# A gated delta rule with an FP4 feed-forward on one core: beta put into the decays, the last output norm on VectorE and ScalarE, and four weight strips decoded before the constants

## The reference

```python
beta = sigmoid(xn @ b_w.T + b_bias + beta_bias) * 2.0            # per row and head
g = -exp(A_log) * softplus(xn @ a_w.T + dt_bias)                 # log of the decay
def step(S, inp):                                                # one row, 16 heads
    q_t, k_t, v_t, g_t, b_t = inp
    S = S * exp(g_t)
    mem = einsum('bhk,bhkv->bhv', k_t, S)
    delta = (v_t - mem) * b_t
    S = S + einsum('bhk,bhv->bhkv', k_t, delta)
    return S, einsum('bhk,bhkv->bhv', q_t, S)
o = o * rsqrt(mean(o * o, axis=-1) + eps)                        # the output norm
o = (o * silu(g_out)) @ o_w.T
# ffn: h = silu(x @ gate) * (x @ up), weights FP4 with scales; y = h @ down; y / rms(y)
```

## Time and profile before

| what | value |
|---|---|
| median of 3 runs | 3336.32 us (3335.82 to 3341.81) |
| profiled execution, its own time | 3332.51 us |
| its span, first to last instruction | 3330.7 us |
| mean granted clock of PE | 0.988 |
| busy: PE, DVE, POOL, ACT | 3142.1, 2390.6, 1918.8, 1667.4 us |
| matmul records | 45632 |
| one step of the loop, from tile to tile | about 101 us |

### The profile page before, as it was taken

How to read it: one execution, slowest core, us unless ns; L and a number is a source line. 1 busy time by engine, 2 the same in 40 slices (tenths; PEclk the granted TensorE clock), 3 DMA queues, 4 the chain that set the end, 5 groups by cost and what they waited for, 6 DMA issues and landing times.

```text
span 3330.7 us, 118645 instructions
## 1 busy us (share of the span) xinstructions
PE 3142.1 (94%) x45632; PEld 2252.9 (68%) x45632; DVE 2390.6 (72%) x5408; ACT 1667.4 (50%) x3306; POOL 1918.8 (58%) x2865
## 2 busy tenths in 40 slices
PE   5999999999999999999999999999999999999995
PEld 4666766766666766666767767667667666767663
DVE  7677776777776777777777767777767777767772
ACT  3544554544554545554445545445545455544452
POOL 4566555666555665556665556665556655556652
PEclk8999999999999999999999999999999999999996
DMA  3111111111111111111111111111111111111111
GB/s 112 39 46 27 37 43 33 46 45 28 34 43 36 46 37 27 43 37 42 46 27 37 43 33 46 46 27 37 43 33 46 40 28 39 42 37 46 34 25 30
DMA packets 318318, 132.08 MB, mean 40 GB/s; under 512 B 277089, under 2 KB 278881, under 8 KB 317793
## 3 DMA queue, kind: packets, MB, share of 16 engines
q1 hardware_dynamic: 313824, 119.26, 14.3%
q10 hardware_dynamic: 4096, 6.42, 0.5%
HBM read 75.30 MB, written 50.33 MB: 38 GB/s over the span
## 4 chain that ended last, share of the span: by engine, by line
PE 77%; DVE 12%; issue 6%; POOL 2%; ACT 1%; ACTq 1%; DMA 1%; DVEq 0%; SPq 0%; POOLq 0%
PE PS L1166 17%; PE PS L1122 13%; PE PS L1153 8%; PE PS L1235 7%; PE PS L1154 7%; PE PS L1376 6%; DVE arena L893 4%; PE PS L1221 3%; PE PS L1300 2%; PE PS L1253 2%; DVE arena L378 2%; PE PS L1271 2%; PE PS L1391 2%; DVE arena L988 1%; PE PS L1178 1%
## 5 line engine op out<-in xcount | busy, mean ns | idle before, releaser
L893 DVE SCALAR_TENSOR_TENSOR arena<-PS,sc,arena 128x256 f32<-128x256 f32 x2112 | 1001.0, 482 | 253.0 <-ACT arena L613 152.2
L1153 PE MATMUL PS<-xh,wgu 128*128 128x256 f32 x2816 | 871.6, 341 | 35.9 <-DVE arena L893 35.4
L613 ACT ACTIVATE arena<-PS,sc 128x256 f32<-128x256 f32 x704 | 330.0, 474 | 759.0 <-PE PS L1154 700.3
L1154 PE MATMUL PS<-xl,wgu 128*128 128x256 f32 x2816 | 698.8, 282 | 0.0
L1166 PE MATMUL PS<-wdn,inner 128*128 128x512 f32 x1408 | 650.7, 592 | 0.0
L1153 PEld LDWEIGHTS PS<-xh,wgu 128*128 128x128 f32 x2816 | 531.2, 189 | 155.8 <-issue 84.2
L511 POOL TENSOR_TENSOR work<-arena 128x31 f32<-128x31 f32 (+15 forms) x992 | 511.9, 516 | 137.5 <-DMA arena<-scr_a 62.3
L515 POOL TENSOR_TENSOR arena<-arena,work 128x31 f32<-128x31 f32 (+15 forms) x992 | 542.1, 546 | 77.7
L1154 PEld LDWEIGHTS PS<-xl,wgu 128*128 128x128 f32 x2816 | 530.4, 188 | 83.2 <-issue 83.2
L1122 PE MATMUL PS<-xnT,wqkv 128*128 128x256 f32 x2048 | 485.6, 388 | 25.2 <-ACT inner L593 15.4
L1122 PEld LDWEIGHTS PS<-xnT,wqkv 128*128 128x128 f32 x2048 | 383.6, 192 | 93.1 <-ACT inner L593 16.4
(11 more groups left out here) (147 smaller groups left out, 4619.2 us busy)
## 6 DMA issues: line engine op xcount, KB each, us to landing
xt<-in_x SPq DMA_DIRECT2D x64, 256.0 KB, 2.8
scr_a<-arena SPq DMA_DIRECT2D x64, 256.0 KB, 2.4
arena<-scr_a SPq DMA_DIRECT2D x256, 64.0 KB, 3.2
obuf<-in_x SPq DMA_DIRECT2D x64, 256.0 KB, 2.8
scr_t<-arena SPq DMA_DIRECT2D x32, 512.0 KB, 2.7
arena<-scr_t SPq DMA_DIRECT2D x256, 64.0 KB, 2.3
out<-obuf SPq DMA_DIRECT2D x64, 256.0 KB, 2.0
wqkv<-in_wqkv ACTq DMA_DIRECT2D x1, 2048.0 KB, 14.3
```

The lines of the kernel that those rows point to most:

```text
L613: eng.activation(fa[:, u % 4, :], PS[:, bank(u, 0), 0:NB * P], ACT.Copy, scale=sc[:, u % 2, KB * m:KB * m + 1]).then_inc(fa_scaled.sem, 1)
L893: eng.scalar_tensor_tensor(out=fa[:, u % 4, :], in0=PS[:, bank(u, k // 2), k % 2 * NB * P:][:, 0:NB * P], scalar=sc[:, u % 2, KB * m + k:K ...
L1153: eng.matmul(o, w, xh[:, k, :], start=True, stop=False)
L1154: ins = eng.matmul(o, w, xl[:, k, :], start=False, stop=True)
```

## The change

Three edits at once.

1. Beta leaves the keys and becomes a factor of E. POOL multiplies E by beta, two instructions of 128x512, in a new `decays_with_beta` between `rest_of_x` and `next_tile`; `gram_products` waits for them. DVE loses the ckb multiply of each batch. PE loses `turn_kb`, and `turn_kqn(1)` takes its place in the order. ACT copies the plain keys of batch b in `masked_keys(b)` in place of `other_keys`.
2. In the last step alone the output norm moves from POOL to DVE (gate and scale) and ACT (logarithm and exponential in place of the power).
3. DVE decodes strips 0 to 3 in a row and makes the constants' products behind them.

```diff
+        def decays_with_beta(eng, n):
+
+            hold(eng, *beta_part.at(n, 3))
+            hold(eng, *decay_done.at(n, NB))
+            for b in range(NB):
+                eng.tensor_tensor(E[:, b, :, :], E[:, b, :, :], bc(bet[:, b, :], CH), ALU.mult).then_inc(e_scaled.sem, 1)
...
                 rest_of_x(eng, n)
+                decays_with_beta(eng, n)
                 next_tile(eng, t, n)
                 keys_for_state(eng, t, n)
-            if t:
+            if t and n:
                 gated_and_scaled(eng, t)
...
                 eng.wait_ge(*kqn_turned.at(n, b + 1))
+                eng.activation(kbT[:, b, :, :].rearrange("p f t -> p (f t)"), PS[:, 6, 2 * P:4 * P],
+                               ACT.Copy).then_inc(kb_copied.sem, 1)
...
-            def other_keys():
...
+            def last_roots():
+
+                eng.wait_ge(*so_done.at(t, NB))
+                eng.activation(ro[:, :, :], so[:, :, :], ACT.Ln, scale=1.0 / DV, bias=epso[:, :]).then_inc(ro_done.sem, 1)
+                eng.preload_act_table_set(EXP)
+                eng.wait_ge(*ro_done.at(t, 1))
+                eng.activation(ro[:, :, :], ro[:, :, :], ACT.Exp, scale=-0.5).then_inc(ro_done.sem, 1)
...
             u_rows(3)
-            other_keys()
+            masked_keys(1)
             gate_copy(0)
             gate_copy(1)
-            masked_keys(1)
...
                 put(eng, kqn[:, b, :].rearrange("p (h d) -> p h d", d=DK), rows(b), cn[:, b, :]).then_inc(qk_part.sem, 1)
-                put(eng, kbq[:, b, 0:C // 2].rearrange("p (h d) -> p h d", d=DK), rows(b)[:, H:, :],
-                    ckb[:, b, :]).then_inc(qk_part.sem, 1)
...
-                eng.wait_ge(*decay_done.at(n, b + 1))
+                eng.wait_ge(*e_scaled.at(n, b + 1))
...
             if not n:
+                for b in range(NB):
+                    eng.wait_ge(*gs_done.at(t, 1))
+                    eng.tensor_tensor(sq[:, b, :], sq[:, b, :], gs[:, b, :], ALU.mult).then_inc(o_gated.sem, 1)
+                for b in range(NB):
+                    eng.wait_ge(*ro_done.at(t, 2))
+                    eng.wait_ge(*o_gated.at(t, b + 1))
+                    oh = sq[:, b, :].rearrange("p (h v) -> p h v", v=DV)
+                    eng.tensor_tensor(oh, oh, bc(ro[:, b, :], DV), ALU.mult).then_inc(o_scaled.sem, 1)
...
-            for i in range(2):
+            for i in range(KB):
                 decode(eng, i)
             eng.wait_ge(consts_loaded.sem, 16 * 11)
...
-            for i in range(2, KB):
-                decode(eng, i)
...
-            turn_kb()
+            turn_kqn(1)
...
             p_times_u(0)
-            turn_kqn(1)
             turn_q()
```

More of the change, by code:

```diff
@@ L130, in build @@
         eps = sb("eps", [P, 1])
+        epso = sb("epso", [P, 1])
         mhalf = sb("mhalf", [P, NB, H])
@@ L213, in build @@
         gx_done = signal("gx_done", 2)
+        e_scaled = signal("e_scaled", 2)
         exs_moved = signal("exs_moved", 1)
@@ L243, in build @@
         knq_copied = signal("knq_copied", 4)
-        kb_copied = signal("kb_copied", 1)
+        kb_copied = signal("kb_copied", 2)
         q_copied = signal("q_copied", 1)
@@ L272, in build @@
         coef_done = signal("coef_done", 6)
-        qk_part = signal("qk_part", 4)
+        qk_part = signal("qk_part", 2)
         qk_done = signal("qk_done", 2)
@@ L303, in build @@
         kqn_turned = signal("kqn_turned", 2)
-        kb_turned = signal("kb_turned", 1)
         q_turned = signal("q_turned", 1)
@@ L665, in masked_keys @@
                                    ACT.Copy, scale=par[:, e:e + 1]).then_inc(knq_copied.sem, 1)
-            def other_keys():
-                if not n:
-                    return
-                eng.wait_ge(*kb_turned.at(n, 1))
-                eng.activation(kbT[:, :, :, :].rearrange("p b f t -> p (b f t)"), PS[:, 6, :], ACT.Copy).then_inc(kb_copied.sem, 1)
             def queries():
@@ L755, in act_step @@
             decay(1)
+            if not n:
+                eng.preload_act_table_set(LOG)
             u_rows(2)
@@ L777, in act_step @@
             unit(3)
-            eng.preload_act_table_set(SILU)
             if n:
+                eng.preload_act_table_set(SILU)
                 gate(0)
@@ L791, in act_step @@
             if not n:
+                last_roots()
                 o_columns()
@@ L826, in _ @@
             eng.preload_act_table_set(EXP)
-            eng.wait_ge(zeroed.sem, 4)
+            eng.wait_ge(zeroed.sem, 5)
             first = Tile(0, 0, first=True)
@@ L1078, in _ @@
             eng.memset(halo[:, :, :, :], 0.0).then_inc(zeroed.sem, 1)
+            eng.memset(epso[:, :], float(np.finfo(np.float32).eps)).then_inc(zeroed.sem, 1)
             eng.memset(S[:, :, :, :, :], 0.0).then_inc(zeroed.sem, 1)
@@ L1309, in turn_kqn @@
                 if b:
-                    eng.wait_ge(*kb_copied.at(n, 1))
+                    eng.wait_ge(*knq_copied.at(n, 2))
                 else:
@@ L1315, in turn_kqn @@
                 ins.then_inc(kqn_turned.sem, 1)
-            def turn_kb():
-                if not n:
-                    return
-                eng.wait_ge(*qk_done.at(n, NB))
-                eng.wait_ge(*knq_copied.at(n, 2))
-                for m in range(4):
-                    ins = eng.transpose(PS[:, 6, m * P:(m + 1) * P], kbq[:, m // 2, m % 2 * P:(m % 2 + 1) * P], ident[:, :])
-                ins.then_inc(kb_turned.sem, 1)
             def turn_q():
@@ L1342, in gram @@
                 hold(eng, *knq_copied.at(n, 2 * (b + 1)))
-                hold(eng, *kb_copied.at(n, 1))
+                hold(eng, *kb_copied.at(n, b + 1))
                 if b:
```

## The result

The changed kernel takes 3348.28 us (median of 17 runs, 3343.91 to 3350.50), the one before 3339.85 us on the same chip (17 runs, 3335.50 to 3345.04). The ratio is 1.0023, 95% interval 1.0016 to 1.0031: slower, by 8 us, where the prediction had 28. The profiled execution after took 3344.44 us with a span of 3342.6, against 3332.51 and 3330.7 before: +11.9.

What follows compares the result with a forecast made beforehand. PE bounds 78 us of a step, DVE the other 22. Steps +40 (30 x 1.33 - 0.2 + 0.3), start -6.2 and last step -5.4 gave +28 on the profiled 3332.51; time given as 3363 us, range 3328 to 3388.

Steps and rivals of the forecast that it cites:

- The picture of two stretches: One loop step: PE sets the pace for 78 us, DVE for the 22 us before it.
- a microsecond on either is a microsecond a step: PE's part up to k_times_u(3) and DVE's part from there: time added or saved on either counts fully.
- The toll, "1.55 us later": In state(3), POOL's E multiplies hold DVE's updates of S, so the layer norm's apply starts 1.55 us later.
- E0: POOL's first E multiply (E1 the second), behind rest_of_x: from 1686.26 to about 1687.5, 0.18 lost to the update.
- The ckb multiply leaves DVE: In products(0), PE's 0.23 us wait for DVE goes: a gain of 0.22 us a step, not 0.84.
- turn_kb leaves PE: Four transposes go behind p_times_u(0), where PE waits anyhow: 0; worth 0.6 if that cover were gone.
- A step, +1.33: Each of 30 loop steps gets longer: 1.55 us of toll less 0.22 for the ckb multiply.
- The step with n = 31: No layer norm ahead, so rest_of_x and E are done before state(3): only -0.2 us.
- Rival 4: PE's granted clock drops when its idle time in the 22 us grows to 5; adds to the forecast; chance 0.05.
- Start and end: Ahead of the loop, earlier strips give -6.2 us; in the last step, the norm off POOL gives -5.4.
- Rival 2: Half the toll in state(3), 0.9 us, as DVE's second update slips in before E0: +9, 3345; chance 0.15.
- Rivals 1 and 3: State(3): no toll, 3317, chance 0.2; or POOL does both E multiplies in a row, 2.2 a step, 3384, chance 0.1.

Runs made afterwards that it cites:

- e7: The changed kernel with both E multiplies behind conv(6) and POOL's rest_of_x moved ahead of layer_norm_scale; ratio to before 0.9921, 3305.03 us.
- e3: The changed kernel with POOL's two E multiplies moved behind the last convolution, conv(6); ratio to before 0.9934, 3312.83 us.
- e5: The changed kernel with only batch 1's E multiply moved behind conv(6), batch 0's left in place; ratio to before 0.9999.
- e10: e7 with turn_kqn(1) and ScalarE's copy of it back at their places of before, behind p_times_u(0); ratio to before 0.9921.
- e6: e3 with four small memsets added at the start of VectorE's program, which only shift its later instructions; ratio to before 0.9945.
- e8: e7 with four small memsets added at the start of VectorE's program; ratio to before 0.9931.

## Why the prediction came out as it did

*The picture of two stretches* held: the 78 us did not change, the loop's loss lies in the 22 us, and the small gain at products(0). But "a microsecond on either is a microsecond a step" is only half true. It holds for a microsecond more on VectorE; for 1.6 fewer, e7 shows a gain of 0.11. The prediction read DVE's chain without a hole as DVE alone being late, and didn't ask how close the next engine was. The nine additions give it away: 4.78 before, in the mean as in the earlier trace rows, and 4.59 for the same nine in every step after. The 0.20 were small waits for ScalarE behind PE, and they came back once DVE was later; in e3, where it is not, they are there (4.75).

*The toll, "1.55 us later"*: this is the step that failed, as a size: it measured 1.19. Together with the 0.20 us that came back in the additions it is why a step forecast at +1.33 came out at +0.67. The mechanism is right, in its place, its order (one update let through per multiply) and its condition (two SBUF operands; the masked multiply out of PSUM passes). Two terms of its working were wrong. "0.18 lost to the update": E0 starts 2.31 us behind rest_of_x's start and lasts 1.04, so POOL loses nothing while DVE's held update finishes 0.08 behind it. "The first update of batch 1 then waits for E1 (1687.5 to 1688.7)": E1 starts with E0's end, 1.00 us behind E0's start, while DVE is at its held update and the masked multiply, and nearly half of it is over when that update arrives (0.48 of 1.05 us). Worked out with this, from rest_of_x's start: its end, 2.35, two multiplies at 1.00 start to start, 0.08, and the last update's 0.19 make 4.62, where the last update of S ends in the trace at 4.63 and in before at 3.46: 1.17. e5 splits the same sum into 0.81 and 0.36. The Trainium skill (SBUF — State Buffer, Who interferes with whom) calls the shared port pair an exclusive lock that the first to issue has for the whole instruction; the trace agrees (held updates end 0.08 us behind POOL's instruction), and shows beside it that at an instruction's end the waiting one gets in at no cost to the other engine.

*"The ckb multiply leaves DVE", -0.22*: right. PE's wait for products(0) went from 8.5 us to 0.8, and from the start of y_times_s(0) to the end of k_times_u(3) the mean fell from 17.65 to 17.43.

*"turn_kb leaves PE", 0*: right against before (k_times_u(3) ends 4.98 behind k_times_u(2) before, 4.96 after), and e10 shows beside it that the place of the other set is worth 0.02. What the four transposes are worth with the cover gone, 0.6 by the prediction, was not tried by itself. Of the 0.44 us a step that e3 gains on before, 0.39 lie between the end of the down products and the next k_times_u(3) (mean 37.92 to 37.53), and some 0.2 of these in the part from y_times_s(0) on, where the ckb multiply was waited for; the rest, ahead of it, comes and goes between kernels (e6 doesn't have it) and is open.

*A step, +1.33*: in means over the 29 steps, 1.19 at apply, +1.00 left at the end of the additions, +0.96 at the end of the down products, and -0.29 behind them, in all +0.67. PE's idle time in the 22 us, forecast at about 5, is 3.67. Of the 0.66 that the forecast is above it, 0.36 is the toll's size and 0.20 the small waits that came back; the remaining 0.10 is spread thin.

*The step with n = 31, "only -0.2"*: wrong by the 4.6 us above the usual toll. That rest_of_x and E are done before state(3) there is right. What happened, a stop of 2.23 us in DVE's issue and the clock that followed, no row of before could have told. It goes with the code's position, as e6 and e8 show (103.53 in place of 106.45, 102.88 in place of 106.50). Not all of the 4.6 is this stop: 3.4 lie in chunks 1 and 2, behind it, and 1.4 ahead of y_times_s(0), where PE has a stop on "issue" of 1.09 us of its own (0.2 less elsewhere); the memsets take away 2.9 and 3.6, and what is left in e6 and e8 is open. That the stop is an instruction fetch is argued from the times of the transfers beside it, and not shown.

*Rival 4, the clock*: "No row shows a drop from waits this short." Now one does: 2.39 us idle, once, and PE at 0.50 for 3.4 us. In the 30 steps, with idle spread over 22 us, the clock stays at 1.00 as forecast.

*Start and end*: -6.2 and -5.4 forecast (its own terms give -5.5), -7.55 (with the first step, for which +0.3 was given) and -5.18 measured; PE's last wait went down by 5.59. Right, as far as it can be told: among the kernels with the new end the last column goes from 123.25 to 127.88, so that the closeness of 5.18 is in part luck, and the wait's 5.59 is the surer number.

The sum by these, from 28.4: the 30 steps -19.9 (30 x 0.66), the step with n = 31 +4.8 (4.6, and the -0.2 given for it), the start -1.65, the end +0.2, in all 11.9, as in the spans. Two sums of the forecast are off by themselves: 3361 and 3.8 make 3365 and not 3363, and tolls of 1.2 and 1.9 on the median of 3336 make 3354 and 3375, not 3350 and 3374. Rival 2 (toll 0.9, +9) came nearest, by luck: no second update slips in ahead of E0, as its case has it, and the +8 is made of a toll of 1.19 that is paid in part. Rivals 1 and 3 are out: there is a toll, and an update is let through between the multiplies.

## What to carry to other kernels

Before an elementwise operation is put on GpSimd, look at what VectorE does at that minute: beside instructions with two SBUF operands it costs what is left of it when the next such instruction arrives, beside instructions that read PSUM it is free. Moving it by some 6 us within the same queue was worth 30 us here, more than the change's own gains. And when an engine's chain has no hole, ask which engine comes next and by how much, since that is all that a gain on the first can bring; small waits inside a group (4.78 against 4.59 for nine additions) are the sign of it, and a wait that lies beneath the chain today (PE's stops on "issue" in p_times_u, 23.9 us in all after the change) is the limit once it is shorter.

The best kernel here keeps all parts of the change, with the multiplies behind the last convolution (e3, 3312.83 us against 3334.75 of before beside it) and rest_of_x early (e7, 3305.03 against 3332.64): 0.66% and 0.79% less than before, with intervals that overlap.

## What the runs showed of the hardware that was not expected

- A GpSimd multiply of 128x512 with a held VectorE instruction beside it takes the same time as one without (2.05 us for two beside the updates of S, 2.06 beside PSUM additions). The held one ends 0.08 us behind it.
- VectorE's own issue can stop for 2.2 us outside of any wait, once, where the code is new to it (the loop's copy for the last tile). With PE's clock behind it the step was 2.9 to 3.6 us longer; four small instructions at the start of its program removed it. In eight kernels it ended 1.71 to 1.74 us behind the start of an 8 KB packet of an instruction queue.
- PE stops on "issue" within p_times_u, for 0.2 to 0.9 us in the full steps and with other lengths from kernel to kernel and step to step; each of 329 such stops ended 2.1 to 3.0 us behind the start of a 16 KB packet of an instruction queue. Where VectorE isn't last, the end of the additions moves with them. Four small instructions on VectorE went with +0.26 us a step on one kernel and 0.01 on another, so a difference of under 0.3% between two orders of this kernel need not come from the order. The cause of that 0.26 stays open.
